# Column tiles for the router mean and the attention's values, and a rearranged end of the graph attention

## The reference, cut to what matters

```python
# graph attention, each layer
e = jax.nn.leaky_relu(alpha_s[src] + alpha_d[dst], NEG_SLOPE)
...
out = jax.ops.segment_sum(msg, dst, num_segments=n)
# weighted graph block, later: the same edges with weights
norm = dinv[row] * ew * dinv[col]
# first feed-forward block: the "tail"
spec_out = feats_c @ out_w + out_b
return ffn_out + bk_scale * spec_out
# router and attention of the last block
g = jnp.mean(e[:, RESERVE:, :], axis=1, keepdims=True)
f = jnp.concatenate([e, jnp.broadcast_to(g, e.shape)], axis=-1)
h1 = _gelu(f @ r_o1_w.T + r_o1_b)
...
o = jnp.einsum('bhqk,bhkd->bhqd', s, v).transpose(0, 2, 1, 3).reshape(B, N, DIM)
```

## Time and profile before

| | |
|---|---|
| median of 3 runs | 361.51 us (361.35 to 361.68) |
| the profiled execution, whole | 362.06 us |
| its span, first to last instruction | 360.2 us |
| PE busy | 349.9 us, 97% |
| DVE, ACT, POOL busy | 180.3, 66.9, 38.4 us |
| DMA | 90.19 MB, mean 250 GB/s |

### The profile page before, as it was taken

One profiled execution on the slowest core, in us unless ns is written; L12 is line 12 of the kernel. 1 busy time (PEld: TensorE's weight loads), 2 busy tenths in 40 slices (PEclk: granted clock), 3 DMA queues, 4 the chain that ended last, 5 costly groups with the idle time before them and its releaser, 6 DMA issues.

```text
span 360.2 us, 4274 instructions
## 1 busy us (share of the span) xinstructions
PE 349.9 (97%) x1628; PEld 222.4 (62%) x1633; DVE 180.3 (50%) x545; ACT 66.9 (19%) x156; POOL 38.4 (11%) x62
## 2 busy tenths in 40 slices
PE   7999999999999999999899999999999999999997
PEld 3566666666565656545455655674545699967754
DVE  3946336485838385466743735424742501163431
ACT  2002111111010111011110321022224401064020
POOL 4900000020000001122031000040130100000000
DMA  8999999998953949999995476775470800000001
GB/s 274 417 368 435 421 415 430 423 407 307 353 233 119 415 144 417 418 397 425 377 397 154 188 265 249 262 278 170 209 265 25 306 2 3 0 2 0 2 0 44
DMA packets 10502, 90.19 MB, mean 250 GB/s; under 512 B 2169, under 2 KB 2822, under 8 KB 6386
## 3 DMA queue, kind: packets, MB, share of 16 engines
q1 hardware_dynamic: 8238, 84.91, 59.4%
q0 software_dynamic: 848, 3.61, 3.0%
q10 hardware_dynamic: 1396, 1.40, 1.1%
HBM read 89.53 MB, written 0.39 MB: 250 GB/s over the span
## 4 chain that ended last, share of the span: by engine, by line
PE 82%; DMA 10%; DVE 4%; SPq 2%; issue 1%; POOL 1%; ACT 0%; DVEq 0%
PE ps L1493 15%; PE ps L1459 14%; PE ps L1865 8%; PE ps L1438 7%; DMA ring<-in_l_wu 6%; PE ps L1685 4%; PE ps L1666 4%; DMA ring<-in_gat_w 3%; PE ps L1481 3%; PE ps L1777 2%; PE ps L1949 2%; PE ps L1921 2%; PE ps L1969 2%; PE ps L1559 2%; PE ps L1500 1%; DVE stats L720 1%
## 5 line engine op out<-in xcount | busy, mean ns | idle before, releaser
L1459 PE MATMUL ps<-ring,xT 128*128 128x512 f32 (+1 forms) x168 | 56.7, 486 | 0.1
L1493 PE MATMUL ps<-ring,h 128*128 128x512 f32 (+1 forms) x168 | 55.6, 486 | 0.0
L1493 PEld LDWEIGHTS ps<-ring,h 128*128 128x128 f32 x168 | 31.2, 190 | 21.9 <-issue 20.1
L1459 PEld LDWEIGHTS ps<-ring,xT 128*128 128x128 f32 x168 | 30.8, 191 | 19.2 <-issue 16.8
L786 DVE CUSTOM_DVE_ANT_0 g<-h,avec 128x768 f32<-128x768 f32 x8 | 7.7, 958 | 35.2 <-ACT h L495 22.2
L495 ACT ACTIVATE h<-ps 128x768 f32<-128x768 f32 (+6 forms) x24 | 13.6, 576 | 61.5 <-PE ps L1459 16.2
L1438 PE MATMUL ps<-ring,xT 128*128 128x512 f32 (+1 forms) x72 | 24.1, 488 | 0.1
L874 DVE TENSOR_SCALAR ring<-ring,idxb,ewb 128x128 bf16<-128x128 bf16 x99 | 24.1, 324 | 0.0
L1370 PE MATMUL ps<-shiftm 128*128 128x512 bf16 x61 | 18.7, 429 | 3.6 <-POOL shiftm L386 2.1
L380 POOL TENSOR_TENSOR rstd<-var,mhalf 128x1 f32<-128x1 f32 x8 | 4.6, 577 | 142.1 <-DVE var L728 69.4
L1438 PEld LDWEIGHTS ps<-ring,xT 128*128 128x128 f32 x72 | 13.4, 190 | 9.3 <-issue 8.4
(11 more groups left out here) (395 smaller groups left out, 511.5 us busy)
## 6 DMA issues: line engine op xcount, KB each, us to landing
ring<-in_gat_w SPq DMA_DIRECT2D x15, 2304.0 KB, 11.7
avec<-in_gat_a SPq DMA_DIRECT2D x9, 768.0 KB, 10.1
ring<-in_l_w SPq DMA_DIRECT2D x3, 2304.0 KB, 15.5
ring<-in_gat_w SPq DMA_DIRECT2D x6, 384.0 KB, 6.0
ring<-in_l_w SPq DMA_DIRECT2D x2, 1152.0 KB, 12.7
ring<-in_l1f_w1a SPq DMA_DIRECT2D x1, 2304.0 KB, 12.7
ring<-in_l1f_w1b SPq DMA_DIRECT2D x1, 2304.0 KB, 10.6
ring<-in_l1f_w2a SPq DMA_DIRECT2D x1, 2304.0 KB, 11.9
```

The costliest lines, as they stand in the source:

```text
L1459: last = mm(ps[:, at + lo:at + hi], xT[:, c, :], w[:, c, lo:hi], start=(c == 0), stop=(c == C - 1))
L1493: last = mm(ps[:, 4 * WIN + lo:4 * WIN + hi], h2[:, par * D + c * P:par * D + (c + 1) * P], w[:, c, lo:hi], start=(n == 0 and c == 0), sto ...
```

## The change

- The score row is a turning (`tr`) instead of a matmul with the identity.
- The edge sum stands in four parts: 6, 8, 15 and 4 matmuls, the last 4 behind the rows, with 9 fillers instead of 11 after them.
- DVE's work on the weighted adjacency moves behind the residual, the centring and the copy of the transposes.
- POOL makes the tail product when head 8's alphas are ready, ahead of its small memsets; the norm's power goes ahead of the degree's.
- SP loads `U_L2` ahead of the two units `U_L1W2A` and `U_L1W2B`; it is now the one that waits for the edges.
- The router mean's share is made by four column tiles of 32 rows in one round, each for a quarter of the contraction; ACT scales the result, and one matmul with ones for each output adds it.
- Each pair of heads' value products stands in two column tiles of 64 rows of one bank; three copies of 256 columns replace the even and odd ones. Values, probabilities' turnings and their additions go in two halves, interleaved.

```diff
@@ -259,6 +259,8 @@
+        mean_rows = h2[:, 0:RHD]
...
         def even(at, n):
@@ -347,14 +349,14 @@
-            for u in range(1, len(UNITS)):
-                if u == 1:
+            for u in (U_L1, U_L1W1A, U_L1W1B, U_L2, U_L1W2A, U_L1W2B, *range(U_L3A, len(UNITS))):
+                if u == U_L1:
                     sp.wait_ge(S["hprod"], 8)
-                if u == 2:
+                if u == U_L1W1A:
                     sp.wait_ge(S["w2_used"], 7)
-                if u == 3:
+                if u == U_L1W1B:
                     sp.wait_ge(S["hprod"], 9)
-                if u == 4:
+                if u == U_L2:
                     sp.wait_ge(s("edges_summed"), 1)
@@ -434,7 +436,10 @@
-            pool.wait_ge(S["hprod"], 9)
+            pool.wait_ge(s("spec_in"), 32)
+            pool.wait_ge(S["alpha_ready"], 9)
+            link(pool.memset(g3[:], 0.0))
+            pool.tensor_tensor(g3[0:11, :], g2[0:11, :], g1[0:11, :], ALU.mult).then_inc(s("tail_ready"), 1)
             link(pool.memset(state, 0.0))
@@ -445,12 +450,8 @@
             pool.memset(combT[:], 0.0).then_inc(s("bk_const"), 1)
+            inverse_root(2)
             inverse_degree_root(1)
-            inverse_root(2)
-            pool.wait_ge(s("spec_in"), 32)
-            pool.wait_ge(S["alpha_ready"], 9)
-            link(pool.memset(g3[:], 0.0))
-            pool.tensor_tensor(g3[0:11, :], g2[0:11, :], g1[0:11, :], ALU.mult).then_inc(s("tail_ready"), 1)
             load_row(avec[:], "l1_b1", 2 * D)
@@ -667,6 +668,8 @@
                     .then_inc(s("eT_ready"), 1)
+            act.wait_ge(s("mean_ps"), 1)
+            nc.scalar.activation(mean_rows, bank(0), ACT.Copy, scale=1.0 / BIT).then_inc(s("mean_copied"), 1)
             for f in range(4):
@@ -686,10 +689,10 @@
                 copy(h2[:, g * 512:(g + 1) * 512], bank((4, 5, 3)[g])).then_inc(s("pT_ready"), 1)
-            o_ps = ps[:, 0:AH * P].rearrange("p (c b n) -> p c b n", b=2, n=P)
-            for n, (lo, hi) in enumerate(((0, 4), (4, C))):
+            for n in (0, 2):
                 act.wait_ge(s("oT_ps"), n + 1)
-                copy(xT[0:AD, lo:hi, :], o_ps[0:AD, lo:hi, 0, :]).then_inc(s("o_even_ready"), 1)
+                copy(xT[:, 2 * n:2 * n + 2, :], bank(n, 2 * P).rearrange("p (c n) -> p c n", n=P)) \
+                    .then_inc(s("o_outer_ready"), 1)
             nc.scalar.activation(cell("scrap"), mhalf[:], ACT.Gelu)
@@ -909,11 +912,6 @@
-            dve.wait_ge(s("edges_summed"), 1)
-            link(nc.vector.tensor_tensor(adj2T[:], bank(3, P, P), ident, ALU.add))
-            link(nc.vector.tensor_tensor(adj2T[:], adj2T[:], bank(3, P, 2 * P), ALU.add))
-            link(nc.vector.tensor_tensor(adj2T[:], adj2T[:], bank(3, P, 3 * P), ALU.add))
-            half_adjacency(1, adj2T)
@@ -938,6 +936,11 @@
             part_T(2)
+            dve.wait_ge(s("edges_summed"), 1)
+            link(nc.vector.tensor_tensor(adj2T[:], bank(3, P, P), ident, ALU.add))
+            link(nc.vector.tensor_tensor(adj2T[:], adj2T[:], bank(3, P, 2 * P), ALU.add))
+            link(nc.vector.tensor_tensor(adj2T[:], adj2T[:], bank(3, P, 3 * P), ALU.add))
+            half_adjacency(1, adj2T)
@@ -1301,17 +1304,22 @@
                     .then_inc(s("p_ready"), 1)
-            dve.wait_ge(s("v_ps"), 1)
+            def heads_values(n):
...
+                lo, hi = HALVES[n]
+                dve.wait_ge(s("v_ps"), n + 1)
+                nc.vector.tensor_tensor(g4[:, lo:hi], ps[:, 6 * WIN + lo:6 * WIN + hi], avec[:, D + lo:D + hi], ALU.add) \
+                    .then_inc(s("v_ready"), 1)
...
             dve.wait_ge(s("in_bv"), 16)
-            nc.vector.tensor_tensor(g4[:], ps[:, 6 * WIN:6 * WIN + D], avec[:, D:2 * D], ALU.add).then_inc(s("v_ready"), 1)
...
+            heads_values(0)
             dve.wait_ge(s("in_bo"), 16)
...
                                                 op1=ALU.add))
-            o_ps = ps[:, 0:AH * P].rearrange("p (c b n) -> p c b n", b=2, n=P)
-            for n, (lo, hi) in enumerate(((0, 4), (4, C))):
-                dve.wait_ge(s("oT_ps"), n + 1)
-                nc.vector.tensor_copy(xT[AD:P, lo:hi, :], o_ps[AD:P, lo:hi, 1, :]).then_inc(s("o_odd_ready"), 1)
+            heads_values(1)
+            dve.wait_ge(s("oT_ps"), 2)
+            nc.vector.tensor_copy(xT[:, 2:4, :], bank(1, 2 * P).rearrange("p (c n) -> p c n", n=P)) \
+                .then_inc(s("o_inner_ready"), 1)
             for n, (lo, hi) in enumerate(HALVES):
@@ -1464,7 +1472,7 @@
                 wait(pe, "z_ready", h)
-                mm(bank(7, P, 256), alpha[:, par, 0:1].broadcast_to([P, P]), ident, start=True, stop=True) \
+                tr(bank(7, P, 256), alpha[:, par, 0:1].broadcast_to([P, P]), ident) \
                     .then_inc(s("score_row_ps"), 1)
@@ -1549,7 +1557,7 @@
             pe.wait_ge(s("ew_rows"), 5)
-            sum_edges(range(0, 10))
+            sum_edges(range(0, 6))
@@ -1559,18 +1567,18 @@
                 last.then_inc(s(signal), 1)
-            sum_edges(range(10, 18))
+            sum_edges(range(6, 14))
             score_row(8, 0)
-            sum_edges(range(18, EC)).then_inc(s("edges_summed"), 1)
+            sum_edges(range(14, 29))
             turn_attention(8)
...
-            wait(pe, "attnT_ready", 9)
-            warm_until(11, "var_ready", 2)
+            sum_edges(range(29, EC)).then_inc(s("edges_summed"), 1)
+            warm_until(9, "var_ready", 2)
             stay_warm(1)
@@ -1886,12 +1894,20 @@
             gmean = cell("router_mean", 4)
...
-            def node_or_mean(c):
...
-                return h1[:, c * P:(c + 1) * P] if c < 4 else gmean[:, c - 4:c - 3].broadcast_to([P, P])
...
-            product_T(unit(U_RO1, "r_o1", "p (c n) -> p c n", c=8), 6, 4, node_or_mean, "ro1_ps", emptied="h1T_ready")
+            w = unit(U_RO1, "r_o1", "p (c n) -> p c n", c=8)
+            for t in range(4):
+                last = mm(ps[t * BIT:(t + 1) * BIT, 0:RHD], gmean[:, t:t + 1].broadcast_to([P, BIT]), w[:, 4 + t, :],
+                          start=True, stop=True, tile_position=(0, t * BIT))
+            last.then_inc(s("mean_ps"), 1)
+            for o in range(4):
+                if o >= 2:
+                    pe.wait_ge(s("h1T_ready"), o - 1)
+                for c in range(4):
+                    mm(bank(6 + o % 2, P), w[:, c, o * P:(o + 1) * P], h1[:, c * P:(c + 1) * P], start=(c == 0), stop=False)
+                if o == 0:
+                    pe.wait_ge(s("mean_copied"), 1)
+                mm(bank(6 + o % 2, P), mean_rows[:, o * P:(o + 1) * P], ones[:], start=False, stop=True) \
+                    .then_inc(s("ro1_ps"), 1)
             wait_unit(pe, U_K)
@@ -1912,6 +1928,13 @@
                         last.then_inc(s("s_ps"), 1)
...
+            def turn_probabilities(g):
...
+                pe.wait_ge(s("p_ready"), g + 1)
+                for h in range(4):
+                    last_ = tr(bank((4, 5, 3)[g], P, h * P), h1[:, (4 * g + h) * P:(4 * g + h + 1) * P], ident)
+                last_.then_inc(s("pT_ps"), 1)
@@ -1922,30 +1945,43 @@
                         scores()
-            last.then_inc(s("v_ps"), 1)
-            pT_banks = (4, 5, 3)
-            for g in range(3):
-                pe.wait_ge(s("p_ready"), g + 1)
-                for h in range(4):
-                    last = tr(bank(pT_banks[g], P, h * P), h1[:, (4 * g + h) * P:(4 * g + h + 1) * P], ident)
-                last.then_inc(s("pT_ps"), 1)
+                    if lo > 0 and c == 2:
+                        turn_probabilities(1)
+                last.then_inc(s("v_ps"), 1)
+                if lo == 0:
+                    turn_probabilities(0)
+            turn_probabilities(2)
...
+            def out_at(c):
...
+                return bank(c // 2, P, c % 2 * P)
...
+            def heads_out(c):
...
+                for half in range(2):
+                    at = POSITION[2 * c + half]
+                    last_ = mm(out_at(c)[half * AD:(half + 1) * AD],
+                               g4[:, c * P + half * AD:c * P + (half + 1) * AD], h2[:, at * P:(at + 1) * P],
+                               start=True, stop=True, tile_position=(0, half * AD))
+                return last_
             pe.wait_ge(s("v_ready"), 1)
-            for at in range(AH):
-                h = POSITION.index(at)
-                if at % 4 == 0:
-                    pe.wait_ge(s("pT_ready"), at // 4 + 1)
-                last = mm(ps[:, h * P:(h + 1) * P], g4[:, (h // 2) * P:(h // 2 + 1) * P], h2[:, at * P:(at + 1) * P],
-                          start=True, stop=True)
-                if at in (7, 11):
+            pe.wait_ge(s("pT_ready"), 2)
+            for c in range(C):
+                if c == 4:
+                    pe.wait_ge(s("v_ready"), 2)
+                    pe.wait_ge(s("pT_ready"), 3)
+                last = heads_out(c)
+                if c % 2:
                     last.then_inc(s("oT_ps"), 1)
...
                     if lo == 0 and c in (0, 4):
```

(5 more changed lines are left out.)

## The result

The changed kernel takes 358.11 us (median of 4 runs, 357.80 to 358.55) beside 361.47 us for the kernel before on the same chip: a ratio of 0.9895, 95% interval 0.987 to 0.992, 3.36 us faster. Six more runs of it later gave 358.38 us (0.988, 0.984 to 0.992). The prediction was 357.5 us (356.1 to 358.7), faster with a chance of 0.94. The profiled execution went from 362.06 to 358.23 us, its span from 360.2 to 356.4 us: 3.8 us, where the sum said 4.03.

A forecast was written before the change was run, and what follows sets the result against it. TensorE was taken as the bound nearly everywhere touched, except head 8's softmax and a weight load. Terms 0.66 + 0.65 + 0.16 - 1.0 + 0.05 + 0.45 + 1.66 + 1.4 gave 4.03 us off the 361.51 median: 357.5 us, range 356.1 to 358.7.

The forecast's parts named there:

- without overlap: Rival: column tiles at router mean and values don't overlap, losing 2.67 and 1.4 us; about 361.5 us, chance 0.03.
- with an emptied PE: Rival: each of four tile-shape changes empties PE, at 0.22 us each, 0.9 off the gain; 358.4 us, chance 0.04.
- with a falling clock: Rival: PE's clock falls to 1.2 GHz while it waits for head 8's held softmax; 362.5 us, chance 0.02.
- Score row: Heads 2 to 7: one pass instead of two saves 0.11 us in each, 0.66 us in all.
- Edge sum: Four fewer matmuls ahead of the last head's second product gain 0.65 us; DVE's activation ends 0.09 before PE needs it.
- Head 8's row: Last head's score row, covered by nothing: a turning takes 0.33 instead of 0.49, so softmax and filler come 0.16 us earlier.
- POOL's coming first: Rival at head 8: second softmax step waits the full 1.8 us, or the reduction is held too; 358.3 us, chance 0.22.
- Tail product on POOL: Head 8's softmax: POOL's two-input product holds DVE's fourth step, a cost of 1.0 us, bounds 0 and 1.8.
- Rows and residual: After the rows, before the transposes: PE's fillers come last, 2.85 us of work instead of 2.89; gain 0.05 us.
- Loads: Before the tail product: with the unit loaded earlier, six turnings run under DVE's coefficient copy; 0.45 us, bounds 0 and 0.55.
- Router mean: Router: 20 matmuls and four column tiles replace 32 matmuls, saving 1.76 us, less 0.1 for ACT's copy: 1.66 us.
- Values: Last attention: value products in two column tiles take 1.40 us instead of 2.82; gain 1.4 us, bounds 0 and 1.48.

The follow-up runs named there:

- Ten edges: First part of the edge sum has ten matmuls again (parts 10, 8, 11, 4), against the changed kernel: 359.27 us, ratio 0.993.
- a seventh: Seven edges instead of six ahead of the last head's second product, tried with three other edits on the changed kernel: together 357.12 us, ratio 0.985.
- old order: Two second-layer units of layer 1 loaded ahead of the layer 2 unit again, edge sum still late, against the changed kernel: 360.06 us, ratio 0.994.
- the fourth edit above: One matmul of the router's second output put ahead of the first mean product, with three other edits on the changed kernel: together 357.12 us, ratio 0.985.
- The run with one tile: All twelve value products of the last attention in the first column tile, output not the reference's, against the changed kernel: 360.78 us in a single run.
- score product: Score row made as a matmul with the identity again, all else as in the changed kernel: 361.01 us, ratio 0.996.
- doubled tail product: POOL makes the tail product twice, one behind the other, at the changed kernel's place: 359.69 us, ratio 0.995.

## Why the prediction was right, point by point

- **Direction and mechanisms**: all eight terms have the right sign, though for the rows and the residual the mechanism was another than the one given, and the rivals without overlap, with an emptied PE and with a falling clock didn't occur in the changed kernel (mean clock 0.999 or 1.000 in its ten runs).
- **Score row**: 0.63 for 0.66, in another way than counted. Head 1 gave 0.16 that I had not counted; the fourth gave nothing (it took 0.08 more), since there the turning waited for a softmax that POOL's row sum had delayed. I had that row (DVE's 1.86 us) and used it as a price, without asking what it held up at its own place. The other heads gave 0.08 to 0.12 each.
- **Edge sum**: 0.36 for 0.65. The step that failed is "with 0.09 to spare": I set the end of DVE's activation against the end of the edges and left out the handover. DVE's activation ends at 141.90 (140.94 + 0.96) and the product begins at 142.04, when TensorE has done its edges. Its first weight load begins 0.03 us ahead of it (142.01), where it was 0.16 before (142.78 for a product at 142.94), and the product takes 7.98 us instead of 7.74. Ten edges cost 0.35, a seventh nothing. DVE after, and the product in the chain before:

```profile
140.94 0.96 DVE L830 SCALAR_TENSOR_TENSOR h<-g 128x768 f32<-128x768 f32 x1 [0.91 <-ACT g L537]
```

```profile
143.11 7.74 PE ps L1559 x24
```

- **Head 8's row**: its 0.16 was put down as a gain that adds up. It is in truth what decides a race: without it POOL comes first and holds DVE 1.58 us instead of 0.74. The prediction had called these starts close and given POOL's coming first a chance of 0.22; that the change fell on the good side by 0.08 us is luck. Parts of a change that share an event can't be summed.
- **Tail product on POOL**: the mechanism and the step held are as forecast, 0.77 for 1.0. The 1.0 had POOL's product begin when DVE's second step had ended; it began inside that step, at 152.21 (the step lasts to 152.42), took 1.88 instead of 1.79 and so ended earlier than counted. The step is held until POOL's product has ended and the reduction before it is not held, so the rule of the Trainium skill (GPSIMD Engine Reference, Key points), contention with instructions that have two SBUF inputs or a two-port mode, is what the trace shows here; the other runs add that a float32 tensor_scalar is held as well (128 columns, 1.56 us, and 14 columns, 1.43) and a one-column reciprocal is not (0.17).
- **Rows and residual**: 0.24 for 0.05. I took TensorE's fillers as what ended last; in the trace before, the last filler had waited 0.23 us for DVE's variance, which stood behind the adjacency. That wait went with it. This was read from the traces, not tried. PE before:

```profile
159.94 0.39 PE L1370 MATMUL ps<-shiftm 128*128 128x512 bf16 x1 [0.23 <-DVE var L741]
```

- **Loads**: 0.41 for 0.45 as a difference of the two kernels. But the two edits belong together: with the late edge sum and the old order the wait is 1.2 us, and in two of four executions the clock fell.
- **Router mean**: 1.49 for 1.66. The tiles took 0.99 for 0.93, and the first four matmuls behind them 1.00 from start to start (298.07 to 299.07) where a later output's take 0.90 (299.29 to 300.19); the chain above, which goes from end to end, has 1.09 and 0.89. The matmuls ahead of the tiles lose 0.08 too: from the first of them to the next product it was 8.05 us before (289.81 to 297.86) and is 8.13 (288.95 to 297.08). I had put a tenth down to ACT's copy, and that wait did not occur: the fourth edit above moved work into that place and changed nothing. So the losses stand at the two switches of tile shape; that the switch is their cause was not tried by itself. PE after:

```profile
298.07 1.16 PE L1906 MATMUL ps<-h,ring 128*128 128x128 f32 x8
299.07 0.39 PE L1909 MATMUL ps<-ones,h 128*128 128x128 f32 x2
299.29 1.06 PE L1906 MATMUL ps<-h,ring 128*128 128x128 f32 x8
300.19 0.39 PE L1909 MATMUL ps<-ones,h 128*128 128x128 f32 x2
```

The Trainium skill (TensorEngine Tiling (Array Packing), Key Properties) states that a change of the tiling mode drains TensorE; from start to start that is at most about 0.1 us on either side here, not the 0.22 of the rival.

- **Values**: 1.48 for 1.40, and the upper bound (which works out as 1.47, 2.82 less half of 12 x 0.2248). The run with one tile puts 1.30 of it down to the overlap; where the other 0.18 arose was not tried.
- **From the sum to the median**: the terms sum to 0.19 more than the traces show. That this is so little is in part luck: five stretches gave 0.69 less than forecast (the start among them, with 0.16), three gave 0.50 more. And 358.0 for the profiled execution was 358.23. I then took 0.5 us off because the profiled execution before lay that far above its median; the one after lay 0.1 above its own. Most of the miss against 357.5 is this step: where that excess of one execution sits was never found.

## What to carry to other kernels

Before moving work to an engine that is free, look at what the other engine does at that moment: here a two-input product of GpSimd of 1.8 us held VectorE's two-input steps and its tensor_scalars until it ended, while a reduction with one input ran on beside it, and a microsecond later it cost nothing, since VectorE waited anyway. Where two parts of a change start from the same event, price them as a race and not as a sum; undoing one part here cost more than three times the 0.82 us counted for it. And look at the granted clock behind every place where TensorE waits: with four edge matmuls fewer under that softmax it fell to half in two of six executions, and in none of five with four fillers there. These are too few to show that the fillers did it, but they cost nothing where TensorE waits anyway.

## What the hardware showed that I had not expected

In some executions TensorE's clock fell from 2.4 to 1.2 GHz for some 3 to 4 us, which makes a mean of 0.995 over the span. The three profiles that caught it show TensorE waiting in one piece shortly ahead of the fall: 1.22 us (old order), 1.42 (ten edges), 1.58 (score product). Falls of the mean clock to 0.995 or less, by kernel:

| kernel | longest wait of TensorE between 150 and 182 us, in its profile | executions with 0.995 or less |
|---|---|---|
| doubled tail product | 2.02 | 2 of 10 |
| score product | 1.58 | 5 of 9 |
| ten edges | 1.42 | 2 of 6 |
| old order | 1.22 | 2 of 4 |
| the kernel after and the other versions | at most 0.78 | 0 of 36 (one with 0.998) |
| the kernel before | 0.44 | 3 of 42 |

So the length of the wait isn't all. The longest one had only 2 falls in 10, and the kernel before, which has no such wait in its profile, fell in three of eleven executions on one chip (364.43 to 365.05 us) and in none of 31 on two others. No trace was kept of those three; where their clock fell, and what else decides it, stays open.

The start of an execution, to the turning of head 0, varied by 0.83 us between profiles (24.09 to 24.92), as much as the runs of one kernel spread; edits worth a few tenths had to be read from distances in the trace.
